# Mask products of the narrow attention scores in four 64-column parts

## The reference

```python
x = _layernorm(x + _L0_attn_ref(x, ...), axis=-1)      # 16 heads of 8, rotary, causal
x = _layernorm(x + _L0_xattn_ref(x, ctx, ctx, mask, ...), axis=-1)   # 16 heads of 8, key mask, fill -1e9
x = _layernorm(x + _L0_ffn_ref(x, ...), axis=-1)       # 8 experts, the best 2 for each token
x = _layernorm(x + _L1_attn_ref(x, ...), axis=-1)      # 16 heads of 64, no mask
x = _layernorm(x + _L1_xattn_ref(x, ctx, ctx, mask, ...), axis=-1)   # 16 heads of 8, key mask, fill -1e12
x = _layernorm(x + _L1_ffn_ref(x, ...), axis=-1)       # ternary weights
```

```python
att = jnp.where(causal, att, jnp.finfo(att.dtype).min)           # _L0_attn_ref
scores = jnp.where(mask == 0, jnp.float32(-1000000000.0), scores) # _L0_xattn_ref
scores = jnp.where(mask == 0, jnp.float32(NEG), scores)          # _L1_xattn_ref, NEG = -1e12
```

## Time and profile before

| | us |
|---|---|
| median of 3 runs | 386.26 (385.08 to 386.55) |
| the profiled execution | 389.23 |
| its span, first to last instruction | 387.4 |
| PE busy | 341.5 (88%) |
| DVE busy | 250.6 (65%) |
| ACT busy | 183.7 (47%) |
| POOL busy | 186.1 (48%) |

### The profile page before, as it was taken

The page is one execution under the profiler, slowest core; times in us unless marked ns, Lnnn a source line. Parts: engine busy times, 40 slices in busy tenths (PEclk is TensorE's granted clock), DMA queues, the critical chain, the costliest instruction groups (busy, mean ns, idle before and its releaser), DMA issues.

```text
span 387.4 us, 9800 instructions
## 1 busy us (share of the span) xinstructions
PE 341.5 (88%) x3718; PEld 265.5 (69%) x3718; DVE 250.6 (65%) x592; ACT 183.7 (47%) x385; POOL 186.1 (48%) x267
## 2 busy tenths in 40 slices
PE   3789899998997089999996798999999999999982
PEld 2556566764897079999995665677777657766662
DVE  1799988888535413573335277845666668886894
ACT  2476567764468423233224243544435356667441
POOL 1867756554454515553313755311212465463673
PEclk9999999999579669999999699999999999999998
DMA  6799930000057111112111110000000000000000
GB/s 195 208 317 254 296 139 2 2 3 2 28 160 217 37 45 48 50 41 56 36 30 34 42 36 15 0 3 2 0 3 3 2 0 3 2 2 3 3 27 27
DMA packets 35938, 22.95 MB, mean 59 GB/s; under 512 B 4142, under 2 KB 33846, under 8 KB 35766
## 3 DMA queue, kind: packets, MB, share of 16 engines
q1 hardware_dynamic: 34582, 19.63, 17.6%
q0 software_dynamic: 1024, 2.10, 1.8%
q10 hardware_dynamic: 288, 0.62, 0.5%
HBM read 14.60 MB, written 7.73 MB: 58 GB/s over the span
## 4 chain that ended last, share of the span: by engine, by line
PE 67%; DVE 12%; issue 7%; POOL 6%; DMA 3%; ACT 2%; SPq 1%; POOLq 0%; DVEq 0%; ACTq 0%
PE banks L427 7%; PE banks L825 7%; PE banks L812 7%; PE banks L547 6%; PE banks L1505 6%; PE banks L1513 6%; PE banks L1536 5%; PE banks L524 4%; PE banks L856 3%; PE banks L1312 2%; PE banks L531 2%; POOL KB L671 2%; PE banks L508 2%; PE banks L371 2%; PE banks L496 2%
## 5 line engine op out<-in xcount | busy, mean ns | idle before, releaser
L671 POOL TENSOR_TENSOR KB<-KT,cst 128x512 f32<-128x512 f32 x48 | 49.3, 1047 | 7.4 <-DVE KT L631 5.6
L331 POOL TENSOR_SCALAR ve<-mv 128x1 f32<-128x1 f32 x40 | 10.6, 266 | 86.3 <-DVE mv L326 86.3
L436 ACT ACTIVATE PT<-banks 128x512 f32<-128x512 f32 x64 | 35.0, 595 | 24.5 <-PE banks L427 23.5
L401 DVE TENSOR_REDUCE mx<-banks 128x16 f32<-128x1024 f32 x32 | 38.6, 1207 | 5.4 <-PE banks L531 4.7
L1528 DVE TENSOR_TENSOR PT<-banks,PR 128x512 f32<-128x512 f32 x23 | 15.9, 691 | 40.4 <-PE banks L1513 35.8
L862 ACT ACTIVATE U<-banks 128x512 f32<-128x512 f32 x40 | 23.9, 597 | 38.0 <-PE banks L825 22.6
L1493 POOL COPY U<-WALL 128x1024 f32 x21 | 21.8, 1040 | 37.7 <-PE banks L1513 36.2
L427 PE MATMUL banks<-cst,PR 128*128 128x128 f32 x256 | 36.6, 288 | 0.5 <-POOL PR L891 0.5
L417 ACT ACTIVATE PR<-PR 128x1024 f32<-128x1024 f32 x32 | 33.8, 1057 | 3.4 <-DVE PR L411 3.2
L812 PE MATMUL banks<-XT,WQKV 128*128 128x128 f32 x256 | 33.3, 293 | 0.4 <-ACT XT L1713 0.4
L812 PEld LDWEIGHTS banks<-XT,WQKV 128*128 128x128 f32 x256 | 31.8, 206 | 1.1 <-ACT XT L1713 0.7
(11 more groups left out here) (183 smaller groups left out, 700.2 us busy)
## 6 DMA issues: line engine op xcount, KB each, us to landing
routed_rows<-zero SPq DMA_DIRECT2D x1, 4544.0 KB, 20.4
U<-in_L_ffn_wg_dram SPq DMA_DIRECT2D x8, 256.0 KB, 4.5
U<-in_L_ffn_wu_dram SPq DMA_DIRECT2D x8, 256.0 KB, 4.9
U<-in_L_ffn_wd_dram SPq DMA_DIRECT2D x8, 256.0 KB, 5.4
U<-in_L_attn_W_qkv_dram SPq DMA_DIRECT2D x1, 1536.0 KB, 23.0
XG<-routed_rows SPq DMA_DIRECT2D x23, 64.0 KB, 1.8
routed_rows<-YS SPq DMA_DIRECT2D x23, 64.0 KB, 1.6
cst<-shape_constants ACTq DMA_DIRECT2D x1, 537.0 KB, 4.4
```

The lines of the kernel that those rows point to most:

```text
L401: dve.tensor_reduce(mx[:, n % 2, :], s, AX.X, ALU.max).then_inc(self.max.sem, 1)
L436: act.activation(PT[:, n % 2, 4 * m:4 * m + 4, :].rearrange("p r q -> p (r q)"), PS[:, B_PT + m, :], ACT.Copy).then_inc(self.pt.sem, 1)
L671: pool.tensor_tensor(KB[:, n % 2, b], bc(KT[:, n % 2, b, :], 1, 8), bc(cst[:, C_HEAD:C_HEAD + 8], 2, SEQ), ALU.mult).then_inc(self.kb.sem, 1)
```

## The change

The two mask products of a tile become four, each with 64 columns and the rows of its own group: for the causal mask the 64 x 64 blocks `idb[f, f]` with `caus[f]`, for the key mask six rows that start at partition 64 g. So `fills`, `mrb` and the integer rows `mri` are held twice, at partitions 0 to 5 and 64 to 69; their tiles grow to 70 partitions, three more small DMAs load the rows, and DVE makes the second copy of `fills` and of `mrb`. The waits count one up accordingly.

```diff
@@ constants()
-                c[2 * j + b, col + SEQ * b:col + SEQ * (b + 1)] = part
+                for half in (0, 64):
+                    c[half + 2 * j + b, col + SEQ * b:col + SEQ * (b + 1)] = part
@@ decoder_kernel
-        mrb = sb("mrb", [6, NT, SEQ], BF16)
+        mrb = sb("mrb", [70, NT, SEQ], BF16)
-        fills = sb("fills", [6, 2, P], BF16)
+        fills = sb("fills", [70, 2, P], BF16)
-        mri = U[0:6, 3584:4096].bitcast(I32).rearrange("p (t k) -> p t k", t=NT)
+        mri = U[0:70, 3584:4096].bitcast(I32).rearrange("p (t k) -> p t k", t=NT)
@@ Narrow.s_pe
-                for g in range(2):
-                    o = PS[:, B_S + g, :].rearrange("q (h k) -> q h k", h=8)
-                    if self.fill is None:
-                        m = pe.matmul(o, idb[:, :], bc(caus[:, :], 1, 8), start=False, stop=True)
-                    else:
-                        m = pe.matmul(o, fills[:, self.fill, :], bc(mrb[:, i, :], 1, 8), start=False, stop=True)
+                for b in range(2):
+                    q = slice(64 * b, 64 * b + 64)
+                    for g in range(2):
+                        o = PS[q, B_S + g, :].rearrange("q (h k) -> q h k", h=8)
+                        if self.fill is None:
+                            f = slice(64 * g, 64 * g + 64)
+                            m = pe.matmul(o, idb[f, f], bc(caus[f, :], 1, 8), start=False, stop=True)
+                        else:
+                            f = slice(64 * g, 64 * g + 6)
+                            m = pe.matmul(o, fills[f, self.fill, q], bc(mrb[f, i, :], 1, 8), start=False, stop=True)
@@ Narrow.qk_dve
-                dve.wait_ge(s_mk, 1)
+                dve.wait_ge(s_mk, 2)
@@ masks
-            dve.wait_ge(s_m, 16 * 4)
+            dve.wait_ge(s_m, 16 * 7)
-            dve.tensor_scalar(mrb[:, :, :], mri[:, :, :], 0.0, None, ALU.is_equal).then_inc(s_mk, 1)
+            for f in (slice(0, 6), slice(64, 70)):
+                dve.tensor_scalar(mrb[f, :, :], mri[f, :, :], 0.0, None, ALU.is_equal).then_inc(s_mk, 1)
@@ sync
-            for j in range(3):
-                load(mri[2 * j:2 * j + 2, :, :], mask[:, 0], s_m)
+            for half in (0, 64):
+                for j in range(3):
+                    load(mri[half + 2 * j:half + 2 * j + 2, :, :], mask[:, 0], s_m)
-            sp.wait_ge(s_mk, 1)
+            sp.wait_ge(s_mk, 2)
@@ vector
-            dve.tensor_copy(fills[:, :, :], cst[0:6, C_FILL0:C_FILL0 + 2 * P].rearrange("p (l q) -> p l q", l=2))\
-               .then_inc(s_bfc, 1)
+            for f in (slice(0, 6), slice(64, 70)):
+                dve.tensor_copy(fills[f, :, :], cst[f, C_FILL0:C_FILL0 + 2 * P].rearrange("p (l q) -> p l q", l=2))\
+                   .then_inc(s_bfc, 1)
@@ tensor
-            pe.wait_ge(s_bfc, 1)
+            pe.wait_ge(s_bfc, 2)
```

## The result

| | us |
|---|---|
| before, median of the runs compared | 385.89 (22 runs) |
| after, median | 383.16 (22 runs) |
| ratio | 0.9933, 95% interval 0.9917 to 0.9949: 2.0 to 3.2 us less |
| profiled execution after | 382.02, its span 380.2 |
| PE, DVE busy | 329.8 (87%), 251.1 (66%) |

What follows compares the result with a forecast made beforehand. DVE was taken to bound self0, PE cross0 and cross1. Terms 0.95 + 0.55 + 1.0 - 0.3 = 2.2 us less took the 386.3 us median to 384.1 us, range 381.5 to 387.0.

Steps and rivals of the forecast that it cites:

- the last pair's 0.55: Last tile of cross0: PE holds the chain again; four parts finish before the clock falls, 0.55 us less than 0.96.
- Four parts side by side: Mask products: four parts on four array quarters start within 0.02 us, one stream of 0.21 us replacing two.
- rival C's first form: Mask parts: halves run one after the other, 0.05 us more a key pair, 387.4 us; rival C's whole chance 0.12.
- Key pair, 0.15 us: Key mask of each tile: entry gap kept, 0.37 us from first part to next line, 0.15 us less.
- the 0.05 us for a first load: Key mask on PE: loading the first 64-column weights behind the entry gap is not hidden and costs 0.05 us.
- Rival A: Key mask: no gap between scores and six-row parts, 0.30 us less a pair, 382.6 us; chance 0.12.
- cross0 and cross1: PE-bound stages: cross0 gains 0.95 us (one causal, five key pairs) before its last pair, cross1 1.0.
- At no cost: Second fills copy (0.33 us) hides in DVE's transpose wait; three more DMA issues, last mask row landing at 17.2, cost nothing.
- self0, 0.3 us: DVE-full stage self0: one more is_equal, 0.34 us long, makes the stage 0.3 us longer.
- the causal parts' 0.2: Causal mask pair: no entry gap but a new exit gap, 0.20 us less; one pair, at 52.1, counted.
- rival B: DVE takes over in cross stages, apply step colliding with POOL, or mask late; gain 1 us, 385.3 us; chance 0.21.
- Rival D: Half-clock stretch of 16.6 us behind cross0 changes: 380 us if gone, 387 or 388 if earlier or longer; chance 0.09.

Runs made afterwards that it cites:

- e5: Changed kernel with all four key-mask parts reading rows 0 to 5, the second copy made but unused; 395.37 us, ratio 1.0050 to the kernel before.
- e7: Changed kernel with key-mask parts padded with zeros from 6 to 64 rows and one row operation; 388.99 us, ratio 0.9905 to the kernel before.
- e8: Kernel before with its two unsplit key-mask products zero-padded from 6 to 128 rows, one row operation; 391.28 us, ratio 0.9958 to the kernel before.
- e2: Changed kernel run again unedited; 390.72 us, ratio 0.9974 to the kernel before.
- e12: Changed kernel unedited, a third time, on the third chip; 383.47 us, ratio 0.9920 to the kernel before.
- e6: Changed kernel with one DVE operation over 70 partitions making both mask-row copies, POOL zeroing the rows between; 390.31 us, ratio 0.9937 to the kernel before.
- e4: Changed kernel with the causal mask back to two products, only the key mask in four parts; 391.33 us, ratio 0.9968 to the kernel before.
- e1: Kernel before run again unedited, against itself; 392.68 us, ratio 0.9988.
- e3: Changed kernel with the key mask back to two products, only the causal mask in four parts; 393.80 us, ratio 1.0043 to the kernel before.
- e9: Changed kernel with its two DVE row operations moved from round 2 to round 9; 386.04 us, ratio 0.9981 to the kernel before.
- e11: The e7 kernel again, unedited, on the third chip; 381.14 us, ratio 0.9872 to the kernel before.

## Why the prediction was right, and where it was not

The forecast was 384.1 against 386.3, 2.2 us less; 2.6 came, and "faster" was the likeliest case. Its steps did less well than its sum. The distances hold 1.55 of the 2.6: the key pairs gave more than forecast, self0 took more, and the last pair's 0.55 was not there. What made up for it, about 1 us, stands in no term of the forecast, and so the closeness of the sum is in part luck.

**Four parts side by side: right.** 0.01 us between the starts, 0.02 promised. e5 shows the condition: each part needs its own quarter, so rows of its own. That was rival C's first form, which the changed kernel does not show.

**Key pair, 0.15 us: right in kind, 0.04 too small.** From the first part to L568 it is 0.34, not 0.37. The entry gap was kept, stream and exit gap are as taken. The term that was off is the 0.05 us for a first load that nothing hides, which came from float32 groups: bfloat16 parts show about 0.03 there and 0.01 of starts. The rule of the Trainium skill on the fast weight load (TensorE: Matmul & The Clock Gate, Weight-path perf modes), which the prediction held against the change, spoke of this very load. The trace agrees in kind: a load of 64 columns takes 0.10 us, one of L531's 128 columns 0.09. But only 0.03 of it shows in a group of four. So a tile gives 0.19 to 0.20, and the tiles are 4.99 apart, not 5.03. DVE's wait is 0.29, not 0.35.

**Rival A, no entry gap: rightly set aside.** The prediction had read the earlier trace rows as a gap of 0.09 us where the shape changes. e7 takes it away with 64 rows and gains 0.11, e8 takes the exit away with 128. TensorEngine Tiling (Array Packing), Key Properties, in the Trainium skill says that changing the tiling mode drains TensorE while moving between tiles of one mode does not. Both runs agree. In them a change costs 0.10 to 0.11 us ahead of the six rows and 0.15 behind them, at full clock.

**cross0 and cross1: right in sum.** From the first to the eighth maximum cross1 took 36.24 us and takes 35.20, 1.04 less (1.0 predicted). In cross0 the eighth to the fourteenth lie 1.11 closer where five key pairs had been priced at 0.75. Not all of it is the pairs': in e2 it is 0.95, five times 0.19. The other 0.16 comes back from self0. In the first profile two apply steps meet POOL there and make DVE's eighth maximum late, while PE goes on; in e2 none does. cross0 is 29.99 in the three profiles with such a meeting (the first, e12 and e6) and 30.15 in the two without (e2 and e4). At the fifteenth maximum, counted from the first and with self0's loss in it, the changed kernel is 0.51 ahead (0.65 predicted: 0.95 less 0.3). DVE takes over at L338 at 82.19 with its 1.06 us, as said, and PE then idles 1.75 us ahead of L372.

**At no cost: right.** DVE reaches the integer mask at 18.47 without a wait, so the three loads are not late. Behind the two copies of `fills` DVE waits 0.83 us for the transposes where it waited 1.20, and goes on at 7.70 (before at 7.66), so the second copy is hidden:

```profile
6.23 0.64 DVE L1926 CAST fills<-cst 6x256 bf16<-6x256 f32 x2
7.70 0.69 DVE L284 COPY WT<-banks 128x512 f32<-128x512 f32 x1 [0.83 <-PE banks L271]
```

**The last pair of cross0, 0.55 us: wrong.** Between the first two profiles the term seems to be there: from the fourteenth to the sixteenth maximum it is 12.14 us before and 11.67 after, and the four parts at 94.27 are indeed through before the clock falls at 95.1. But L531's 0.96 us was the price of a half clock that began where it did in this one execution, and I took that stretch for a part of the program. In e1 the kernel before has full clock there until 103.4 and takes 11.71 us. In e12, where the clock falls at 93.8, before the last pair, the changed kernel takes 12.80. At full clock DVE is full through those tiles, so a shorter pair gives 0.04 there and not 0.55. The step that failed is "PE holds the chain again": it does so only where the clock has fallen.

**self0, 0.3 us: far too small.** The distance is 0.60 longer, and the causal parts' 0.2 in the last round is in it, so 0.8 was paid. The first part is the second operation's step: from the start of the row operations to the shuffle behind them 0.90 us in place of 0.34, so 0.56 and not 0.34. I had priced an operation by the start of what follows it; two in a row start 0.44 apart, and the shuffle then starts 0.11 behind its own mask load. The second part is what rival B had named for the cross stages, an apply step that meets POOL, and it came in self0, in two tiles. The rows of POOL and DVE in the kernel before and of POOL after (DVE's row after is shown above):

```profile
40.86 2.09 POOL L671 TENSOR_TENSOR KB<-KT,cst 128x512 f32<-128x512 f32 x2
41.45 0.57 DVE L337 TENSOR_SCALAR X<-R,mv,rstd 128x128 f32<-128x128 f32 x1
```

```profile
41.39 2.04 POOL L676 TENSOR_TENSOR KB<-KT,cst 128x512 f32<-128x512 f32 x2
```

In both the apply step starts while the first of POOL's two is running (41.45 before, 41.52 after) and ends 0.1 us behind it (42.02 and 42.52). It is 0.57 long when POOL began 0.6 us before it, and 1.00 when POOL began 0.1 us before it. In e3 and e5, with two row operations but no such meeting, self0 is 36.99 and 36.93; so the two meetings cost 0.2 to 0.3 in self0, of which cross0 gives 0.16 back. Together 0.56 + 0.24 - 0.2 = 0.6. e6 undoes the first part and one of the meetings. The edit does not fix their number: the changed kernel has two in its first profile and in e12 and none in e2, and e6, e8 and e9 have one.

**The rest.** The distances give 0.60 - 1.11 - 1.04 = -1.55 us. Measured were 2.0 to 3.2 less. About 1 us is left, and the clock may hold most of it. On the third chip, by the mean granted clock of a run:

| granted clock | before | after (e12) |
|---|---|---|
| 0.971 | none | 3 runs, 382.0 to 382.2 |
| 0.962 to 0.968 | 8 runs, 384.4 to 385.6 | 3 runs, 382.8 to 383.2 |
| 0.955 to 0.958 | 9 runs, 386.1 to 388.0 | 4 runs, 383.7 to 384.1 |
| 0.942 to 0.949 | 6 runs, 389.3 to 391.4 | 2 runs, 387.8 to 388.1 |

In the second row, where the levels are most alike, the changed kernel is 1.8 us ahead by the medians, near the 1.55 of the distances. In the next two it is 2.8 and 3.0 ahead, but its clocks there (0.958, 0.945) are mostly higher than those of before (0.955, 0.942). And it reaches a level that the kernel before has in none of its 23 runs there. Rival D said that the clock could move either way, and its sign, a stretch other than 16.6 us, came: 3.4 in the first profile. But it moves from execution to execution, in the kernel before too. Whether the change makes the better levels likelier (0.971 came in six of its 22 runs of the first comparison too) no run here can settle: none sets the clock.

## What to carry to other kernels

A small product between two groups of another shape is paid for by its neighbours: here 0.53 us for 0.44 us of stream, and padding six rows with zeros to the neighbours' 64 made it cheaper, not dearer. Parts that are to run side by side need operands in rows of their own, and where the copies are made, one operation over 70 partitions costs what one over six does (0.42 and 0.41 us), once the rows between are zeroed. How often an operation of another engine is met can change with the execution too, so a distance that holds such a meeting needs a second profile before it is put down to the edit. Before a term is built on a long row, look whether the granted clock in its window is the program's or only that execution's: a second profile of the same kernel tells.

## What was not expected of the hardware

**A wait on two of the chips.** DVE's timeline of e1, at the end of the first stream:

```profile
98.82 0.18 DVE L326 BATCH_NORM_AGGREGATE mv<-stats 128x2 f32<-128x6 f32 x1
101.74 0.26 DVE L657 RECIPROCAL rs<-banks 128x16 f32<-128x16 f32 x1 [2.74 <-remote]
```

("remote" is a release of which the trace has no source.) The reciprocals wait 2.74 us although PE's products for them had ended by 98.6. All eight profiles of the first two chips have such waits on DVE, one or two of 1.6 to 3.3 us, that end between 100 and 117 us; in six of the eight ACT has waits of that size too; the six other profiles have none. In e1 POOL runs the scatters of the routed rows until 100.9. They come with before and after alike. e7 and e11 are one kernel on two chips and place what they cost. Up to the last maximum of cross0 the two profiles are alike (94.10 and 94.04 us from the start). From there to the first product of the experts it is 45.82 us in e7, which has the waits, and 37.98 in e11; behind it they are alike again (246.9 and 247.0 us to the last instruction). That is the 7.8 us between their medians (388.99 and 381.14). The cause of the waits stays open.

**The apply step ends with POOL's operation.** A DVE operation of 0.47 us takes 1.06 where it starts just behind one of POOL's of 1.04 us (82.19 against 82.12), and ends 0.09 us behind it. The Trainium skill's GPSIMD Engine Reference, Specifications, says that POOL's interface to SBUF is shared with VectorE, for vector instructions with two SBUF inputs or in a two-port mode. The lengths fit; which of the two L338 is, no run tested.

**The clock can fall in mid-work.** In e2, e4 and e12 it fell for 3.4 us at 25.5 to 26.4 us, inside self0; from 12.0 to there in e12, PE had been busy 10.2 of 13.5 us. In e12 it costs self0 0.9 us, set against the first profile, which has two meetings with POOL as e12 has; in e2, which has none, 0.9 as well, set against e3 and e5, which have none either (36.99, 36.93). That is more than most of the steps weighed here.
